# Four-layer graph network on one core: the last layer's float16 scale taken from a bound, its last rows split straight from PSUM, its first four output tiles accumulated together

## What is computed

```python
def _gc(x, adj, W, b):
    return adj @ (x @ W) + b
h = relu(_gc(x, adj, W1, b1))      # W1 256 x 512
h = relu(_gc(h, adj, W2, b2))      # W2 512 x 512
out = _gc(h, adj, W3, b3)          # W3 512 x 256
x = layernorm(x + out)
```

## Time and profile before

| | us |
|---|---|
| median of three runs | 831.36 |
| lowest, highest of them | 829.05, 848.21 |
| profiled execution: its time | 831.39 |
| profiled execution: its span | 829.6 |
| TensorE busy in the span | 775.2 |
| VectorE, ScalarE, GpSimd busy | 447.0, 333.3, 115.5 |
| mean granted TensorE clock | 0.986 |

### The profile page before, as it was taken

One profiled execution on the slowest core, in us unless ns is written; L12 is line 12 of the kernel. 1 busy time (PEld: TensorE's weight loads), 2 busy tenths in 40 slices (PEclk: granted clock), 3 DMA queues, 4 the chain that ended last, 5 costly groups with the idle time before them and its releaser, 6 DMA issues.

```text
span 829.6 us, 11863 instructions
## 1 busy us (share of the span) xinstructions
PE 775.2 (93%) x4247; PEld 511.4 (62%) x4288; DVE 447.0 (54%) x937; ACT 333.3 (40%) x499; POOL 115.5 (14%) x214
## 2 busy tenths in 40 slices
PE   7898989899979999999979999999988999997997
PEld 6776656666656978686835554665663456464443
DVE  4586667477867778787873354221225111112655
ACT  4575536554465464646541142331335222223100
POOL 1012111112730001010111120000002000000343
PEclk9999999999989999999999999999999999999999
DMA  8979999995400000000011000000000000000011
GB/s 226 184 128 172 181 180 173 171 200 100 90 1 14 1 1 1 1 2 1 1 32 52 0 1 0 1 0 0 0 1 25 1 1 0 0 0 1 19 39 44
DMA packets 112572, 42.41 MB, mean 51 GB/s; under 512 B 103312, under 2 KB 109584, under 8 KB 112528
## 3 DMA queue, kind: packets, MB, share of 16 engines
q1 hardware_dynamic: 110224, 33.44, 20.6%
q0 software_dynamic: 2304, 8.39, 6.5%
HBM read 22.95 MB, written 2.10 MB: 30 GB/s over the span
## 4 chain that ended last, share of the span: by engine, by line
issue 40%; PE 35%; DVE 7%; SPq 6%; POOL 4%; DMA 4%; ACT 4%; POOLq 0%; ACTq 0%; DVEq 0%
PE ps L664 10%; PE ps L817 6%; PE ps L767 5%; SPq L365 4%; PE ps L571 3%; PE ps L754 3%; DMA turned<-pl 2%; PE ps L530 2%; SPq L358 2%; PE ps L583 2%; POOL rstd L417 1%; PE ps L553 1%; ACT em L855 1%; DVE em L1124 1%; PE ps L585 1%
## 5 line engine op out<-in xcount | busy, mean ns | idle before, releaser
L664 PE MATMUL ps<-adjT,x 128*128 128x512 bf16 (+1 forms) x739 | 168.5, 379 | 8.4 <-DVE x L1361 4.3
L664 PEld LDWEIGHTS ps<-adjT,x 128*128 128x128 f16 x768 | 71.8, 98 | 91.0 <-issue 5.6
L583 PE MATMUL ps<-sup,turned 128*128 128x512 f16 x256 | 85.7, 385 | 4.4 <-DMA turned<-pl 3.8
L1082 DVE TENSOR_TENSOR hh_lo<-hf,hh_hi 128x512 fp32r<-128x512 f32 x32 | 22.1, 692 | 116.6 <-ACT hf L1028 116.6
L789 PE MATMUL ps<-adjT,G 128*128 x375 | 82.6, 379 | 0.9 <-ACT hf L1028 0.4
L689 PE MATMUL ps<-H_hi,es_hi 128*128 128x258 f32 x256 | 76.8, 300 | 2.1 <-DVE es_lo L1082 1.7
L689 PE MATMUL ps<-H_hi,es_lo 128*128 128x258 f32 x256 | 72.4, 283 | 0.0
L689 PE MATMUL ps<-H_lo,es_hi 128*128 128x258 f32 x256 | 72.4, 283 | 0.0
L585 PE MATMUL ps<-sup,turned 128*128 128x256 f16 x256 | 70.6, 276 | 0.0
L416 POOL TENSOR_TENSOR rstd<-mv,epsc 128x1 f32<-128x1 f32 x64 | 14.6, 227 | 369.6 <-DVE mv L1096 361.8
L789 PEld LDWEIGHTS ps<-adjT,G 128*128 128x128 f16 x384 | 37.3, 98 | 45.4 <-issue 0.9
(11 more groups left out here) (196 smaller groups left out, 1439.8 us busy)
## 6 DMA issues: line engine op xcount, KB each, us to landing
adjb<-in_adj POOLq DMA_DIRECT2D x16, 512.0 KB, 7.4
x<-in_x SPq DMA_DIRECT2D x4, 512.0 KB, 6.1
out<-adjf SPq DMA_DIRECT2D x16, 128.0 KB, 1.7
adjf<-in_L_gnn_W SPq DMA_DIRECT2D x1, 1024.0 KB, 5.4
W1f<-in_L_gnn_W SPq DMA_DIRECT2D x1, 512.0 KB, 3.7
adjf<-in_L_gnn_W SPq DMA_DIRECT2D x1, 512.0 KB, 3.8
we<-in_L_gnn_edge_w SPq DMA_DIRECT2D x1, 256.0 KB, 3.8
w0x<-in_L_gnn_weight SPq DMA_DIRECT2D x1, 256.0 KB, 7.0
```

What stands on the lines that cost most here:

```text
L583: ins = mm(bank(6 + u), PT(HI, u)[:, jt, :], sup[:, jt, :], start=(jt == 0), stop=False, skip_group_check=True)
L664: ins = mm(bank(4 + f), x16[:, part, jt, f * P:(f + 1) * P], adj(b, jt), start=(jt == 0 and part == HI), stop=(jt == T - 1 and part == LO))
```

## The change

Five edits, all in the last layer.

1. The maxima are no longer taken of the products with W2 and W3. DVE takes the maximum of h (of `hf`, 128 x 512, L1464 after) right behind each low part, and the largest weight once (`weight_bound`: 128 x 2048 of W2 and 128 x 1024 of W3), which POOL reduces over the partitions. The scale is the largest h times the largest weight times HID over TOP (`bound_scale`): it bounds the product without having seen it. So the scale follows from the last slice of h, and not from the last product. ACT's `hf` writes now wait for the maximum of the slice two before (r_maxed), not for its low part.
2. The last block's four tiles of rows go to four banks (`ROW_BANK` = 2, 3, 0, 1), are not copied, and are split to float16 straight from PSUM.
3. The order of the tiles in both splits and in the products that read them is `ORDER` = 12, 0, 1, 2, 13, 3, 4, 5, 14, 6, 7, 8, 15, 9, 10, 11.
4. The drains of ACT and DVE, which signal h1_done and h2_done, stand behind the splits; PE's stay where they were.
5. The first four output tiles are accumulated together in banks 4 to 7, four matmuls for each input tile. `final3` reads them there. The following tiles use banks 0 and 1 as before, and the first two of them wait for nothing.

```diff
+    STORED = T - TB
+    ORDER = [t for k in range(TB) for t in (STORED + k, 3 * k, 3 * k + 1, 3 * k + 2)]
+    ROW_BANK = (2, 3, 0, 1)
...
+            pool.wait_ge(wmax_ready, 1)
+            nc.gpsimd.partition_all_reduce(wm[:, 0, 1:2], wm[:, 0, 0:1], P, RMAX).then_inc(wmax_all, 1)
             pool.wait_ge(tmax_ready, 2)
...
-            def rows(b, ws, width):
+            def rows(b, ws, width, last=False, uncounted=0):
...
-                    pe.wait_ge(r_copied, 2 + n - 1)
+                    if last and k >= 2:
+                        pe.wait_ge(h_f, 2 + (b + 1) * KH)
+                    else:
+                        pe.wait_ge(r_copied, 2 + n - 1 - uncounted)
+                    to = ROW_BANK[k] if last else 2 + k % 2
...
-            rows(2 * B - 1, W3s, D)
+            rows(2 * B - 1, W3s, D, last=True, uncounted=TB)
             pe.drain().then_inc(h2_done, 1)
+
+            for i, jt in enumerate(ORDER):
+                pe.wait_ge(c3_lo, T + i + 1)
+                for k in range(TB):
+                    ins = mm(bank(4 + k), adjT[:, 0, jt, k * P:(k + 1) * P], f16[:, jt, :], start=(i == 0),
+                             stop=(i == T - 1))
+                    if i == T - 1:
+                        ins.then_inc(o3_mm, 1)
...
-                act.wait_ge(h_lo, 2 + n - 1)
+                act.wait_ge(r_maxed, 2 + n - 1)
...
-            mid(B - 1)
+            for o in range(KH):
+                hidden(B - 1, o, o % 2, b1c, 1.0)
+
+            act.wait_ge(scale_ready, 2)
+            for jt in ORDER:
+                if jt >= STORED:
+                    act.wait_ge(r_mm, jt + 1)
+                    frm = bank(ROW_BANK[jt - STORED], HID)
+                else:
+
+                    if jt >= AHEAD:
+                        act.wait_ge(c3_lo, ORDER.index(jt - AHEAD) + 1)
+                    frm = G[:, jt + AHEAD, :]
+                run(g16(jt, HI), frm, ACT.Copy, scale=g1[:, 2:3]).then_inc(c3_hi, 1)
             act.drain().then_inc(h1_done, 1)
...
                     low(hh[LO][:, o, :], hf[:, o % 2, :], hh[HI][:, o, :]).then_inc(h_lo, 1)
...
+                    nc.vector.reduce_max(gm[:, bass.ds(n - first, 1)], hf[:, o % 2, :], AX_X).then_inc(r_maxed, 1)
+
+            def bound_scale(n):
+
+                dve.wait_ge(wmax_all, n - 1)
+                own.link(ts(wm[:, n - 2, 1:2], wm[:, n - 2, 1:2], HID / TOP, None, ALU.mult))
+                dve.wait_ge(r_maxed, 2 + (n - 1) * T)
                 nc.vector.reduce_max(g1[:, 0:1], gm[:, :], AX_X).then_inc(tmax_ready, 1)
-                scale_of(n)
+                dve.wait_ge(gmax_ready, n)
+                own.link(ts(g1[:, 3:4], g1[:, 1:2], wm[:, n - 2, 1:2], 1e-30, ALU.mult, ALU.max))
+                nc.vector.reciprocal(g1[:, 2:3], g1[:, 3:4]).then_inc(scale_ready, 1)
```

More of the change, by code:

```diff
@@ L155, in build @@
         bab = sb(ctx, "bab", [P, 1, 2])
+        wm = sb(ctx, "wm", [P, 2, 2])
         adjf = sb(ctx, "adjf", [P, 2, HALF])
@@ L780, in _ @@
             hidden1(B - 1)
-            rows(B - 1, W2s, HID)
+            rows(B - 1, W2s, HID, last=True)
             pe.drain().then_inc(h1_done, 1)
@@ L791, in hidden2 @@
                 ins.then_inc(h_mm, 1)
-            for jt in range(T):
-                pe.wait_ge(c3_lo, jt + 1)
+            for i, jt in enumerate(ORDER):
+                pe.wait_ge(c3_lo, i + 1)
                 for o in range(KH):
@@ L798, in _ @@
                         ins = mm(bank(4 + o), g16(jt, part, o * P, P), adj(0, jt),
-                                 start=(jt == 0 and part == HI), stop=(jt == T - 1 and part == LO))
-                    if jt == T - 1:
+                                 start=(i == 0 and part == HI), stop=(i == T - 1 and part == LO))
+                    if i == T - 1:
                         ins.then_inc(h_mm, 1)
@@ L1045, in _ @@
             agg_high(2, B - 1, 1)
-            mid(B - 1)
+            for o in range(KH):
[10 more added lines that the diff above has]
+                run(g16(jt, HI), frm, ACT.Copy, scale=g1[:, 2:3]).then_inc(c3_hi, 1)
             act.drain().then_inc(h1_done, 1)
-            act.wait_ge(scale_ready, 2)
-            for t in range(T):
-                wait_from(act, c3_lo, t - AHEAD + 1)
-                run(g16(t, HI), G[:, t + AHEAD, :], ACT.Copy, scale=g1[:, 2:3]).then_inc(c3_hi, 1)
             act.wait_ge(h1_done, 4)
@@ L1060, in _ @@
                     hidden(B + b, o, 4 + o, b2c, g1[:, 3:4])
-            rows(2 * B - 1, F, -B * TB, D)
+            act.wait_ge(scale_ready, 3)
+            for jt in ORDER:
+                if jt >= STORED:
+                    act.wait_ge(r_mm, T + jt + 1)
+                    frm = bank(ROW_BANK[jt - STORED], D)
+                else:
+                    frm = F[:, jt, :]
+                run(f16[:, jt, 0:D], frm, ACT.Copy, scale=g1[:, 2:3]).then_inc(c3_hi, 1)
             act.drain().then_inc(h2_done, 1)
-            act.wait_ge(scale_ready, 3)
-            for t in range(T):
-                run(f16[:, t, 0:D], F[:, t, :], ACT.Copy, scale=g1[:, 2:3]).then_inc(c3_hi, 1)
         @block.vector
@@ L1446, in _ @@
             hidden_low(B - 1)
[L1447 to L1466 removed]
+            bound_scale(2)
+            for i, jt in enumerate(ORDER):
+                dve.wait_ge(c3_hi, i + 1)
+                frm = bank(ROW_BANK[jt - STORED], HID) if jt >= STORED else G[:, jt + AHEAD, :]
+                stt(g16(jt, LO), frm, g1[:, 2:3], g16(jt, HI), ALU.mult, ALU.subtract).then_inc(c3_lo, 1)
+            dve.drain().then_inc(h1_done, 1)
+            hidden_low(B, T)
+            dve.wait_ge(w3_landed, 16)
+            weight_bound(1, W3f)
+            for b in range(B + 1, 2 * B):
+                hidden_low(b, T)
+            bound_scale(3)
+            for i, jt in enumerate(ORDER):
+                dve.wait_ge(c3_hi, T + i + 1)
+                frm = bank(ROW_BANK[jt - STORED], D) if jt >= STORED else F[:, jt, :]
+                stt(f16[:, jt, D:2 * D], frm, g1[:, 2:3], f16[:, jt, 0:D], ALU.mult, ALU.subtract).then_inc(c3_lo, 1)
+            dve.drain().then_inc(h2_done, 1)
             def final3(t, u):
+                at = 4 + t if isinstance(t, int) and t < TB else u
                 y_free(3 * T + t)
```

66 lines of the change are left out of this document (25 added, 41 removed).

## The result

The changed kernel takes 825.75 us (median of 16 executions, 819.33 to 841.92) against 833.56 us of the kernel before on the same chip (16 executions). The ratio is 0.9923, with a 95% interval of 0.9894 to 0.9951: faster by 0.8%, and not by the 1.1% that was forecast. (The ratio leaves out executions over 1.5% above the fastest of their kernel, so it is not the quotient of the two medians.) The profiled execution took 828.15 us, span 826.3 us.

What follows compares the result with a forecast made beforehand. TensorE, busy 775.2 of 829.6 us, was taken as the bound, with time to win only in gaps and slow stretches. 5.5 + 2.8 + 3.2 - 2.0 = 9.5 us off 831.39 gave 821.9 us, range 818.6 to 827.

Steps and rivals of the forecast that it cites:

- First hand-over: From W2 products to second product: early scale saves 4.0 us of idleness and 1.5 of slow clock, 5.5 us.
- Second hand-over: From W3 products to third product: it starts at 762.4 instead of 765.27, saving 2.8 us.
- Costs laid at nothing: New maxima, W2's weight maximum and W3's later transfer were put at no cost; W3 had 6.8 us of cover.
- C: Rival: POOL's reductions bring the scale 6.8 us late at the hand-overs, time 829.1 us; chance 0.04.
- D: Rival: W3, behind later splits, makes TensorE wait ahead of block 1; 832 us and more; chance 0.02.
- E: Rival: last of the four PSUM products is late in the order, at most 1 us, 822.9; chance 0.15 with B.
- The pacing: First output tile's matmuls wait for split tiles; four matmuls per input tile would remove this, 3.2 us.
- Theory 2: Follow-up theory: bound scale and PSUM splits already give enough lead; four tiles win nothing, their wait and clock are pure loss.
- A wait of 2.0 us that was not there before: Third product: TensorE waits ahead of tile 6 until VectorE has read tile 4; costs 2.0 us, up to 3.
- rival B: Third product: four tiles together gain nothing, VectorE's backlog lasts longer, time 825.8 us; chance 0.15 with E.
- own case: The forecast itself: 9.5 us saved in the last layer, 821.9 us, no slow clock behind the new wait; chance 0.45.
- rival A: Clock falls behind the new wait ahead of tile 6, costing 1.7 us, time 823.6; chance 0.32.

Runs made afterwards that it cites:

- one_tile: Changed kernel with the fifth edit undone, output tiles made one at a time in alternating banks 4 and 5: median 824.01 us, ratio 0.989 to the kernel before.
- written_out: Changed kernel with VectorE's output tiles 2 to 7 written out, its loop beginning at tile 8: 823.94 us, ratio 0.9877 to the kernel before.
- after_again: The changed kernel measured a second time, unaltered: median 826.56 us, ratio 0.9866 to the kernel before.
- two_tiles: Changed kernel with two output tiles accumulated together instead of four, tiles 2 and 3 in banks 6 and 7: median 820.3 us, ratio 0.9808 to the kernel before.
- four_more_banks: Changed kernel with output tiles 4 to 7 in banks 0 to 3, waiting for nothing: median 819.4 us, ratio 0.9841 to the kernel before.
- slice_last: Two output tiles together, plain tile order, fourth-slice W3 products last for the last block, TensorE's second drain removed: 820.74 us, ratio 0.9836 to the kernel before.
- fill: Changed kernel with 11 extra, unread matmuls into bank 2 ahead of TensorE's wait before tile 6: median 825.97 us, ratio 0.989 to the kernel before.
- after_third: The changed kernel measured a third time, unaltered, in one execution: 833.07 us against 835.01 for the kernel before.

## Why the prediction was right and wrong

- *First hand-over, 5.5 us forecast.* It brought 5.8: 4.11 by the start of the second product and 29.49 - 27.80 = 1.69 by the clock that no longer falls. The scale came as laid out. The second product starts 0.10 us behind the end of the last W2 product (625.59 - 625.49), where 0.37 was put for drain and restart. The forecast's "0.23 us after its weight load" and its 29.26 us were the missing record, and almost cancelled.
- *Second hand-over, 2.8 us.* It brought 3.11 (3.49 - 0.38). Of both hand-overs the measured gain is 8.9 us, against 8.3.
- *Costs laid at nothing.* Right: the low parts and maxima of the hidden stage kept pace (W1 to G without its gap is 104.66 us, and was 104.69 before), W2's maximum took 2.27 us, and W3 had 9.7 us of cover where 6.8 were forecast. Rivals C, D and E fell with it: no late scale, no wait for W3, no wait for a product in PSUM.
- *The pacing, 3.2 us, put to the four tiles.* It went, but not by them. one_tile has next to no pacing either. The step had held that four matmuls per input tile give splitting its lead; its first low part starts at 758.00, 2.7 us ahead of X at 760.71, and at 0.40 us for a tile that is lead enough for all but 0.5 us. Theory 2 holds.
- *"A wait of 2.0 us that was not there before."* This is the term that was mis-sized. It was 2.33 us as idleness, and tile 6 starts at X + 23.22 instead of 22.7. DVE's first read came as laid out, at X + 13.4, but its loop start of 0.57 us was missing in the sum; it was mentioned under rival B alone. written_out shows it: without the loop tile 6 starts at X + 22.64.
- *The choice between the own case and rival A* is the step that failed. The clock fell behind the wait in the changed kernel's profile, 1.68 us, which rival A had at 1.7. After the choice it is own case plus 0.6 (hand-overs) less 0.5 (wait) less 1.7: 9.5 - 1.6 = 7.9, measured 8.0. In after_again the clock stood and the last layer was 313.86 - 304.23 = 9.6 us shorter, which is the own case. That it fits to 0.1 us is luck: the hand-overs brought 0.6 more and the wait took 0.5 more than laid out. So both cases happen to one program, and which of them a single profile shows is luck., read as a threshold between 1.83 and 1.96 us, were two rows made to bear too much: the very place of the 1.96 us had no fall behind it in four of the thirteen traces. So the term that the own case put at nothing is a slow stretch of 1.7 us with about an even chance. The Trainium skill (TensorE: Matmul & The Clock Gate, HAM oscillation) lets the clock fall only behind longer gaps than any of these. The falls behind 2.33 and 2.32 us contradict it, as the one behind 1.96 did.
- *B, four tiles together gain nothing,* had 0.15 with E, and was right of the fifth edit, though by less than its price: 65.24 us from X to the end against one_tile's 61.59, and nothing won on the kernel before.
- *"This counts as within 2%."* The forecast held its own gain too small to be told from no change. The interval of 0.9894 to 0.9951 lies wholly below 1, so the gain is small, but told. The last layer's 8.0 us would be 0.990, inside the interval.

In sum: edits 1 and 2 carry the gain (with the fourth, which no run takes out by itself), the third is neutral, and the fifth gives back 3.65 us of what would have been 11.6 (313.86 - 302.22), or 2.0 in an execution where the clock stands (304.23 - 302.22). The stages say that two_tiles, four_more_banks and slice_last are 4.1 to 5.8 us shorter than the changed kernel's profile; their ratios to the kernel before, 0.981 to 0.984, stand 0.3 to 1.2 points under those of the changed kernel (0.9866 and 0.9923), and their intervals overlap in part. What stays open: why the first layer takes up to 13 us more in one execution than in another with the same code, and what decides on the clock behind 2.33 us. That idleness is needed for a fall is well borne out. From the first W1 product to the last matmul the thirteen traces show eight falls, and each begins at or behind a gap of 1.39 us or more. The five runs without such a gap behind X (one_tile, four_more_banks, fill, two_tiles, slice_last) have no fall there.

## What to carry to other kernels

When a chain's head is moved forward, work out again how much lead the consumer has before adding a second remedy for the same wait: the second one here paid for a wait with nothing left to win. Several accumulators that finish together give the engine behind them a backlog; free banks for as many tiles as it needs to catch up, or finish fewer together. And an idle gap of about 2 us on TensorE should be priced with about half the chance of a slow stretch behind it, and not by a sharp threshold: in the last layer the clock fell behind three of six gaps between 1.96 and 2.33 us. And where a first matmul stands one pitch behind its weight load, count the records before reading a gap from it.

## What was not expected of the hardware

- The same program with the same idleness (2.33, 2.33 and 2.32 us) had a clock of 0.53 behind it, then 1.00, then a slow stretch again. In the last layer the clock stood behind gaps of 1.41 (in every run), 1.75, 1.96, 2.08 and 2.33 us, and fell behind 1.39 (with short waits behind it), 2.32 (two runs) and 2.33. Behind the 1.97 us of the earlier trace rows's place it fell in nine of thirteen traces.
- VectorE's start of a loop costs some 0.57 us, which shows as idleness behind its own last instruction.
- TensorE's drain costs 0.26 us between products of 256 columns (0.38 against 0.12 from start to start), once nothing hides it. Behind those of 512 columns it is as much: a gap of 0.49 against a pitch of 0.23.
- The first layer's length differs by up to 13 us between executions. Nearly all of it arises before the first turn of x with the identity behind that layer (215.71 to 228.40 us); from there to the first W1 product it is 295.3 to 297.7 us in the thirteen profiles. after_third had expected 297 at most and measured 297.7.
